# Mixture of experts in the last stage of a decoder kernel: from all tokens through every expert to token rows in expert slots, moved by indirect transfers

## The reference

```python
h = _layernorm(x, ln_g, ln_b).reshape(Tn, D)          # Tn = 1024, D = 128
top_vals, top_idx = jax.lax.top_k(h @ Wr, 2)          # 7 logits a token, 2 kept
gates = jax.nn.softmax(top_vals, axis=-1)
idx = top_idx.T.reshape(-1); gat = gates.T.reshape(-1) # first picks of all, then second picks
onehot = jax.nn.one_hot(idx, 7, dtype=jnp.int32)
pos = jnp.sum(jnp.cumsum(onehot, axis=0) * onehot, axis=-1) - 1
keep = pos < 366                                      # CAPACITY = ceil(1.25 * 1024 * 2 / 7)
xe = zeros((7, 366, D)).at[idx, pos_c].set(h[tok], mode='drop')
ye = einsum('ecf,efd->ecd', silu(xe @ W1) * (xe @ W3), W2)   # F = 512
routed = sum over both picks of ye[idx, pos_c] * (gat * keep)
shared = silu(h @ W1s) * (h @ W3s) @ W2s
x = _layernorm(x + routed + shared)
```

## Time and profile before

| | |
|---|---|
| median of 3 runs | 2568.12 us (2568.01 to 2568.81) |
| the profiled execution: its own time | 2562.91 us |
| its span, first to last instruction | 2561.1 us |
| mean granted TensorE clock | 0.924 of full speed |
| PE busy / DVE busy / ACT busy / POOL busy | 88% / 54% / 45% / 36% |
| the last stage begins at | 2342.3 us |

### The profile page before, as it was taken

The page is one execution under the profiler, slowest core; times in us unless marked ns, Lnnn a source line. Parts: engine busy times, 40 slices in busy tenths (PEclk is TensorE's granted clock), DMA queues, the critical chain, the costliest instruction groups (busy, mean ns, idle before and its releaser), DMA issues. The chain is left out here.

```text
span 2561.1 us, 59784 instructions
## 1 busy us (share of the span) xinstructions
PE 2253.1 (88%) x24643; PEld 1302.8 (51%) x24643; DVE 1380.0 (54%) x3379; ACT 1154.9 (45%) x2603; POOL 909.7 (36%) x807
## 2 busy tenths in 40 slices
PE   4989998799778999999999999985887987997998
PEld 2445666455344555555555555553455434554443
DVE  3544544467356767777677777753543223672333
ACT  1324444135326667676676767661440111363221
POOL 2010000202239878787787878741000002000000
PEclk8989999899679999999999999997886997898998
DMA  2110000000011211111111111100000100000010
GB/s 63 25 32 1 1 1 1 8 11 3 1 53 31 51 31 44 37 42 49 33 50 38 40 39 43 48 17 4 15 1 17 33 16 13 14 2 26 25 37 21
DMA packets 57662, 65.00 MB, mean 25 GB/s; under 512 B 8957, under 2 KB 37285, under 8 KB 57396
## 3 DMA queue, kind: packets, MB, share of 16 engines
q1 hardware_dynamic: 54900, 58.86, 8.9%
q10 hardware_dynamic: 2496, 2.36, 0.4%
HBM read 33.26 MB, written 0.52 MB: 13 GB/s over the span
## 5 line engine op out<-in xcount | busy, mean ns | idle before, releaser
L3340 POOL TENSOR_TENSOR l1fb_rinv<-l1fb_ssq,neghalf 128x8 f32<-128x8 f32 x192 | 316.0, 1646 | 173.8 <-DVE l1fb_ssq L3383 171.2
L3483 ACT ACTIVATE l1fb_p<-ps,l1fb_shift 128x64 f32<-128x64 f32 x768 | 177.7, 315 | 181.0 <-PE ps L3639 136.6
L3342 POOL TENSOR_TENSOR l1fb_qk<-l1fb_qk,l1fb_r 128x512 f32<-128x512 f32 x192 | 244.0, 1271 | 0.0
L3546 PE MATMUL ps<-l1fb_wqkv,l1fb_xs 128*128 128x512 f32 x384 | 217.7, 650 | 20.1 <-issue 10.8
L3344 POOL TENSOR_TENSOR l1fb_qk<-l1fb_qk,l1fb_rinv 128x512 f32<-128x512 f32 x192 | 200.1, 1042 | 15.0
L3393 DVE TENSOR_TENSOR l1fb_r<-ps,l1fb_turn_tab 128x256 f32<-128x256 f32 x384 | 142.8, 413 | 0.0
L3390 DVE TENSOR_TENSOR l1fb_qk<-ps,l1fb_turn_tab 128x512 f32<-128x512 f32 x192 | 132.3, 689 | 14.1 <-POOL l1fb_qk L3342 11.6
L3577 PE MATMUL ps<-ident,l1fb_qk 128*128 128x128 f32 x768 | 118.4, 277 | 20.9 <-issue 15.3
L3491 ACT ACTIVATE l1fb_both<-ps 128x512 f32<-128x512 f32 (+1 forms) x194 | 117.7, 607 | 41.7 <-PE ps L3639 41.1
L3381 DVE TENSOR_REDUCE l1fb_ssq<-l1fb_sq 128x8 f32<-128x512 f32 x192 | 129.7, 676 | 3.4 <-ACT l1fb_sq L3463 3.4
L3463 ACT ACTIVATE l1fb_sq<-ps 128x512 f32<-128x512 f32 x192 | 117.8, 613 | 12.7 <-PE ps L3546 10.6
(11 more groups left out here) (708 smaller groups left out, 5139.7 us busy)
## 6 DMA issues: line engine op xcount, KB each, us to landing
l1fb_v<-l1fb_v SPq DMA_DIRECT2D x48, 260.0 KB, 4.2
l1fb_v<-l1fb_v SPq DMA_DIRECT2D x48, 195.0 KB, 3.9
l1fb_wqkv<-in_L_ffn_Wqkv SPq DMA_DIRECT2D x24, 256.0 KB, 2.8
l3f_w<-in_L_ffn_W SPq DMA_DIRECT2D x21, 256.0 KB, 3.2
l2f_w<-in_L_ffn_W SPq DMA_DIRECT2D x16, 256.0 KB, 3.1
l1fb_wqkv<-in_L_ffn_Wqkv SPq DMA_DIRECT2D x6, 512.0 KB, 4.6
l1fb_wo<-in_L_ffn_Wo SPq DMA_DIRECT2D x6, 512.0 KB, 4.0
l1fb_w<-in_L_ffn_W SPq DMA_DIRECT2D x6, 341.0 KB, 3.0
```

The source lines that it names most:

```text
L3340: nc.gpsimd.tensor_tensor(w.rinv[:, u, :], w.ssq[:, u, :], chip.neghalf[:, 0:8], ALU.pow).then_inc(*w.unit_norm.end(f"rinv{u}"))
L3342: nc.gpsimd.tensor_tensor(w.qk[:, u, :], w.qk[:, u, :], fp(w.r2), ALU.add).then_inc(*w.unit_norm.end(f"add{u}"))
L3483: last = nc.scalar.activation(w.p[:, c % 2, q, j, :], ps[:, SCORE_BANK + j, q * SEEN:(q + 1) * SEEN], ACT.Exp, bias=w.shift[:, c, j, q:q + 1])
L3546: nc.tensor.matmul(ps[:, PROJ_BANK(u), :], w.xs[:, x.odd, q * P:(q + 1) * P], w.wqkv[:, col:col + 512], start=True, stop=True)\
```

## The change

Routed experts no longer run over all tokens. Each has 384 slots (`L3_SLOTS`, 366 rounded up to a multiple of 128). The routing chain on DVE now makes slot numbers as integers: `sent` (where a token's row goes; out of bounds for one that is dropped) and `home` (where its result is read). The path of a token row is: `z` in SBUF, by an indirect transfer that POOL issues to the scratch tensor `xs` in device memory, zeroed at the start of the stage by one SP transfer; 16 such transfers, one for each tile and pick, of 128 rows of 512 bytes. When all have landed SP loads each expert's 384 rows (`xg`), PE turns them (`turn`), ACT applies gain and bias (`hx`). `inner` runs on 384 columns, four units an expert. `rows(r, i)` makes the result as tokens x features, 128 slots at a time, with `midx` as the weights side: 12 matmuls of 128x128 an expert, issued in thirds between the next expert's units. ACT copies them to `yg`, SP stores them to `ys`. When all seven are stored, POOL issues 16 indirect transfers that gather each token's two rows to `back`, and DVE adds shared + gate x row + gate x row. The shared expert's `outer` gives tokens x features too (four 128x128 matmuls a unit, where one 128x512 stood), so nothing is turned back at the end. All experts' weights have buffers of their own, and SP issues their 24 loads at once, behind the zeroing. The exponential of the gates is moved ahead of the first silu on ACT. A constant `c_slots` is loaded with the other constants.

```diff
+    C, K, N = F // P, L3_SLOTS // P, L3_SLOTS
...
-            for r in range(E + 1):
-                if r >= 2:
-                    sp.wait_ge(*mpe.done(f"acc{r - 2}_{n - 1}"))
+            sp.dma_start(xs.rearrange("(i p) d -> p i d", p=P), chip.zeros[:, :].unsqueeze(1).to_broadcast([P, E * K, D]))\
+                .then_inc(emptied, 16)
+            for r in range(E + 1):
...
+            sp.wait_ge(scattered, 16 * 2 * TILES)
+            for r in range(1, E + 1):
+                sp.dma_start(xg[:, r - 1, :, :], xs[(r - 1) * N:r * N, :].rearrange("(i p) d -> p i d", p=P)).then_inc(loaded[r], 16)
+            for r in range(1, E + 1):
+                sp.wait_ge(*yact.done(f"y{r}"))
+                sp.dma_start(ys[(r - 1) * N:r * N, :].rearrange("(i p) d -> p i d", p=P),
+                             yg[:, r - 1, :].rearrange("p (i d) -> p i d", d=D)).then_inc(stored, 16)
...
+            eng.wait_ge(emptied, 16)
+            eng.wait_ge(*cdve.done("sent"))
+            for i in range(2 * TILES):
+                nc.gpsimd.indirect_dma_start(xs, bass.IndirectOffsetOnAxis(ap=sent[:, i:i + 1], axis=0), z[:, i % TILES, :], None,
+                                                bounds_check=E * N - 1, oob_is_err=False)\
+                    .then_inc(scattered, 16)
+            eng.wait_ge(stored, 16 * E)
+            for q in range(TILES):
+                for i in (q, TILES + q):
+                    nc.gpsimd.indirect_dma_start(back[:, i, :], None, ys, bass.IndirectOffsetOnAxis(ap=home[:, i:i + 1], axis=0))\
+                        .then_inc(gathered[q // QT], 16)
...
             for pair in range(B // PAIR):
+                for b in range(PAIR * pair, PAIR * pair + PAIR):
+                    eng.wait_ge(gathered[b], 16 * 2 * QT)
+                    for q in range(b * QT, b * QT + QT):
+                        last = nc.vector.scalar_tensor_tensor(mixedy[:, q, :], back[:, q, :], weight[:, q:q + 1],
+                                                              ps[:, 6 + q // 4, q % 4 * D:q % 4 * D + D], ALU.mult, ALU.add)
...
+                nc.tensor.matmul(ps[:, g % 2, 0:wide(g)], w1[:, r, c * P:(c + 1) * P], moving, start=True, stop=True)
+                nc.tensor.matmul(ps[:, 2 + g % 2, 0:wide(g)], w3[:, r, c * P:(c + 1) * P], moving, start=True, stop=True).then_inc(*mpe.end(f"ab{g}"))
...
+            def rows(r, i):
...
+                for c in range(C):
+                    last = nc.tensor.matmul(ps[:, 5, i * D:(i + 1) * D], midx[:, r % 2, c, i * P:(i + 1) * P], w2[:, r, c, :],
+                                            start=c == 0, stop=c == C - 1)
+                last.then_inc(*mpe.end(f"y{r}_{i}"))
+
+            for g, (r, c, half) in enumerate(work):
+                if g == first(1):
+                    turn(1)
+                inner(g)
+                if 2 <= g < first(1) + 2:
+                    outer(g - 2)
+                if g == 0:
+                    counts()
+                if r > 1 and c:
+                    rows(r - 1, c - 1)
+                if 0 < r < E and c == 2:
+                    turn(r + 1)
+            for i in range(K):
+                rows(E, i)
```

More of the change, by code:

```diff
@@ L2781, in l3_ffn @@
[L2781 to L2786, removed]
+        loaded = [sem(f"loaded{r}") for r in range(E + 1)]
+        emptied, scattered, stored = sem("emptied"), sem("scattered"), sem("stored")
@@ L2898, in _ @@
[L2898 to L2914, removed]
@@ L2985, in outer @@
-            def outer(r, u):
-                c, half = units[u]
-                eng.wait_ge(*mdve.done(f"mid{r}_{u}"))
-                nc.tensor.matmul(ps[:, 6 + half, :], w2[:, r % 2, c, :], mid[:, u % 2, :], start=False, stop=False).then_inc(*mpe.end(f"acc{r}_{u}"))
-            for r in range(E + 1):
-                for u in range(n + 2):
-                    if 0 < r < E and u == n // 2 + 1:
-                        spread(r)
-                    if u < n:
-                        inner(r, u)
-                    if u >= 2:
-                        outer(r, u - 2)
-                    if r == 0 and u == 2:
-                        counts()
-                    if r == 0 and u == 5:
-                        weights_turned()
-                    if r == 0 and u == 6:
-                        spread(0)
@@ new lines, in outer @@
+            def outer(g):
+                r, c, half = work[g]
+                eng.wait_ge(*mdve.done(f"mid{g}"))
+                for i in range(512 // P):
+                    last = nc.tensor.matmul(ps[:, 6 + half, i * D:(i + 1) * D], mid[:, g % 2, i * P:(i + 1) * P], w2[:, 0, c, :],
+                                            start=False, stop=c == C - 1 and i == 512 // P - 1)
+                last.then_inc(*mpe.end(f"acc{g}"))
+            def rows(r, i):
+                if i == 0:
+                    eng.wait_ge(*mdve.done(f"mid{first(r) + C - 1}"))
+                if r == 1:
+                    eng.wait_ge(*cdve.done("pos"))
+                elif i == 0:
+                    eng.wait_ge(*yact.done(f"y{r - 1}"))
+                for c in range(C):
+                    last = nc.tensor.matmul(ps[:, 5, i * D:(i + 1) * D], midx[:, r % 2, c, i * P:(i + 1) * P], w2[:, r, c, :],
+                                            start=c == 0, stop=c == C - 1)
+                last.then_inc(*mpe.end(f"y{r}_{i}"))
```

238 lines of the change are left out of this document (125 added, 113 removed).

## The result

| | kernel before | changed kernel |
|---|---|---|
| median | 2568.07 us (4 runs, 2565.98 to 2568.81) | 2503.95 us (4 runs, 2500.17 to 2506.24) |
| ratio | | 0.9752, 95% interval 0.9736 to 0.9767 |
| profiled execution, span | 2561.1 us | 2503.2 us |
| last stage, from its first transfer's issue to the output's issue | 215.0 us | 150.6 us |

The changed kernel is 64.1 us faster; 2506 us was forecast for it, and 2503.95 measured. The last line of the table is the measure that I use from here on, and I call it the stage. The eleven stages ahead of the last one are not touched by the change, yet the profiled execution reached its last stage at 2349.1 where the kernel before did at 2342.3. The first two experiments show that this is a difference between executions.

What follows compares the result with a forecast made beforehand. The last stage was taken as bound by PE. One chain of slots, scatters, load, experts, store, gathers and close ends at 2498.8 for 2561.1; 2568.1 - 62.3 = 2506 us, range 2472 to 2540.

Steps and rivals of the forecast that it cites:

- slots known: Last stage's routing: after PE's counts, DVE's products, additions and small steps have the slot numbers ready at 2371.5.
- X: Time one indirect transfer of 128 rows holds POOL, in scatters and gathers: 1.25 us, between bounds of 0.40 and 3.4.
- expert 1's first product: PE's first routed product, after scatters, landing, expert 1's load, three turns and one ACT operation: at 2397.7.
- half clock behind PE's return: After PE's stop of 14 us before the experts: 11 us of work at half speed, a loss of 5.6 us.
- first product to the last rows: Seven routed experts on PE: 58.7 us, plus 5.6 us lost to the clock, ending at 2462.0.
- ACT's copy and last store: Behind the last expert: ACT's copy 0.7 us, then SP's last store 3.0 us, to 2465.7.
- sixteen gathers: POOL's transfers after all seven stores: 20.0 us, covered by nothing, to 2485.7.
- close: Behind the gathers: POOL's part, second pair's mixing, output's issue and end of span, 13.1 us, to 2498.8.
- Rival B: Both chains of 16: POOL is held until each transfer lands, X = 3.4, 69 us more, 2575; chance 0.10.
- C: Both POOL chains: X near 2, 24 us more, 2530; chance 0.16.
- D: Both POOL chains: POOL as quick as SP, X = 0.4, total 2473; chance 0.12.
- E: PE's 128x128 matmuls in routed experts and shared `outer` are dearer, 0.42 apart instead of 0.224, total 2524; chance 0.10.

Runs made afterwards that it cites:

- The first two experiments: Both kernels profiled again unchanged: the kernel before 2572.13 us (one run), stage begins 2351.4; the changed kernel 2502.39 us, stage begins 2344.9.

## Why the prediction was right, step by step

The times in the column "measured" are those of the changed kernel's profile less 6.8 us, by which its stage began later:

| step | forecast | measured |
|---|---|---|
| slots known | 2371.5 | 2370.6 |
| X, one transfer on POOL | 1.25 | 1.29 and 1.255 |
| last scatter done | 2391.5 | 2391.9 |
| landing, then load of expert 1 | 2.5 + 2.7 | 1.1 + 2.6 |
| PE's wait | 14 | 13.7 |
| expert 1's first product | 2397.7 | 2397.3 |
| half clock behind PE's return | 11 us | 5.6 us |
| a routed expert | 8.18 | 8.17 |
| first product to the last rows | 58.7 + 5.6 | 61.9 |
| ACT's copy and last store | 0.7 + 3.0 | 2.8 |
| sixteen gathers | 20.0 | 19.8 |
| close | 13.1 | 14.6 |
| end of the span | 2498.8 | 2496.4 |

**The unknown X.** The choice between bounds of 0.40 and 3.4 us was the whole of the uncertainty, and 1.25 was right to 0.04. Its reason was not: I gave POOL "an index for each row" to read, and the run with 64 rows shows 1 ns a row. The price is nearly all fixed per transfer, so the middle of the two bounds hit it by luck. The row of one scatter lasts 0.97 us in the trace, and 0.30 us lie between two. The Trainium skill, "DMA: Bandwidth & Descriptors", section "Latency and other measured facts", gives about 1 us to the first byte on this path; the 0.97 us agree with it. The sum needs the 0.30 us as well.

**Expert 1's first product** came within 0.4 us of the forecast, but out of errors that cancelled. The slots were known 0.9 us early. The first scatter then began 0.95 us behind them (2377.43 to 2378.38), for which I had no term, and the chain took 0.4 us more than 20. The last scatter landed in 1.1 us and not in 2.5. The transposes and ACT's operation took 1.7 us (2402.48 to 2404.14) and not 1.0, being at half clock.

**Rival B** (POOL held until the landing) falls: a transfer starts 1.28 us behind the last, and the last landed 2.10 us behind its own start. **C and D** fall by the same 1.28 us. **E** falls at the 0.89 us for four 128x128 matmuls, 0.223 each, where the forecast had 0.224 from the earlier trace rows.

**The clock** was the term that was mis-sized. That it would be at half behind the wait was right. I carried over the 11 us of the earlier trace rows; it was 5.6 us, and 5.5 to 7.3 in the variants without work put into the wait. The stretch of the earlier trace rows lies in the routing, among other work: there PE came back at 2348.92 and the clock at about 2363.8, 14.8 us later, so even that length was not 11. What makes one return last 14.8 us and the other 5.6, no run shows. Of the 5.6 us, 1.7 lie ahead of the first product and 4.0 behind it, which cost 2.0 us where 5.6 were forecast.

**The PE part**, from that product to the last rows, was 2.4 us shorter than forecast: 3.6 less for the clock, 0.1 more in expert 2, and 1.1 more at the end, for which I had no term. There PE had no other work left and stood for 0.8 us until the last chunk's product (DVE, to 2462.65) and ACT's copy of the rows before (to 2462.95) were done, and the 24 passes ended 0.2 us later than 2.7:

```profile
2462.09 0.56 DVE L2858 TENSOR_TENSOR l3f_midx<-ps,l3f_act 128x384 f32<-128x384 f32 x1 [1.63 <-ACT l3f_act L2962]
2462.46 0.49 ACT L2947 ACTIVATE l3f_yg<-ps 128x384 f32<-128x384 f32 x1 [0.40 <-PE ps L3024]
```

**The store** landed in 2.0 us, not 3.0. I had taken it from loads and from the 512 KB output, when nothing as small and as alone was in the trace.

**The close** took 1.5 us more, as the drain's 2.0 us had no term and the rest came 0.5 us under the sum.

Forecast less measured, the errors are +0.4 us at expert 1, +2.4 more by the last rows, +0.9 at the store, +0.2 at the gathers, -1.5 in the close: 2.4 us in all, where the start of the stage differed between executions by 11. So near a hit is in part luck: X, the clock and the drain could each have missed by more.

## What to carry to other kernels

An indirect transfer is paid by the piece on POOL, 1.25 to 1.29 us here for 128 rows of 512 bytes and hardly less for 64 (1.23), one behind the other: in this range count the transfers of a routing scheme, not their bytes, and look for what lies beside each chain. What a new chain waits for should be made as early as its inputs allow, piece by piece: half of the slots sent before the other half was known was worth 7.9 us, although DVE had more instructions to do for it. In comparing profiles of long programs, measure the changed stage from its own start, since the unchanged part in front of it moved by 11 us between executions.

## What the hardware showed that I had not expected

- The end of the block waits for a drain on POOL although all of its transfers have landed: 2.3 us with 32 transfers, 1.65 with 24, 0.37 when it is not asked for, 0.28 in the kernel without them. It is 2.3 with 64 rows a transfer too, so it goes by their number and not their rows, by (2.3 - 1.65) / 8 = 0.08 us each if it is linear, for which two points say little. These gaps are counted from DVE's last instruction.
- The clock fell from 2.4 to 1.2 GHz in waits of PE of 3.6, 8.6 and 13.6 us, and behind waits of 2.8 and 4.7 us it fell 0.3 and 0.5 us after PE's return. It came back 5.5 to 7.3 us behind that return, with no order by the length of the wait. Where PE had been kept busy up to 1.3 us before its next work, it was at half for 3.4 us. To shorten a wait, or to fill it but for its end, did not avoid the fall.
- The row of an indirect transfer in the trace ends before the data is there: the last scatter's ends at 2398.73 and SP could go on at 2399.86. By the Trainium skill, "Perfetto Trace Analysis", section "DMA Instruction — SWDGE (GPSIMD)", the end is where the last descriptor is written, not where the data has moved; these 1.1 us agree.
